# Moving one-hot compares between three engines in a two-layer graph network kernel

## What is computed

```python
h = relu(layernorm(x))                       # 256 x 512
adj[src, dst] = adj[dst, src] = 1.0          # 256 x 256, plus the identity
dinv = 1 / sqrt(adj.sum(1))
x = x + (adj * dinv[:, None] * dinv[None, :]) @ (h @ weight) + bias
h = relu(layernorm(x))
hs, hv = h[:, :128] @ w_in2f_s, h[:, 128:] @ w_in2f_v         # per node
s, v = hs[dst], hv[dst]                                       # gather to the edges
Wij = (ssp(edge_attr_20 @ W1 + b1) @ W2 + b2) * edge_weight   # per edge
agg = segment_sum(products of (s, v, edge_attr_4, Wij), src)  # scatter to the nodes
x = x + output_layers(agg)
```

## Time and profile before

| | |
|---|---|
| median of 3 runs | 71.9 us (71.62 to 71.95) |
| the profiled execution | 71.83 us, of which 69.8 us are the span of the profile |
| PE busy | 61.7 us (88%) |
| PEld busy | 48.6 us (70%) |
| DVE busy | 60.1 us (86%) |
| ACT busy | 48.6 us (70%) |
| POOL busy | 39.5 us (57%) |

### The profile page before, as it was taken

The page is one execution under the profiler, slowest core; times in us unless marked ns, Lnnn a source line. Parts: engine busy times, 40 slices in busy tenths (PEclk is TensorE's granted clock), DMA queues, the critical chain, the costliest instruction groups (busy, mean ns, idle before and its releaser), DMA issues.

```text
span 69.8 us, 1215 instructions
## 1 busy us (share of the span) xinstructions
PE 61.7 (88%) x407; PEld 48.6 (70%) x407; DVE 60.1 (86%) x124; ACT 48.6 (70%) x74; POOL 39.5 (57%) x46
## 2 busy tenths in 40 slices
PE   3999998999999999897998979999999999998340
PEld 1236754568834268796987969998898989997220
DVE  4599999999979968989999898989898999972760
ACT  0700059978999697967979999988696969732700
POOL 5000030000676989594799979999999988700000
PEclk9999999999999999999999999999999999999995
DMA  0899998984000000000000000000000000000044
GB/s 1 129 396 247 361 499 379 449 317 124 9 0 0 0 0 0 0 0 5 0 0 0 0 0 9 5 0 0 0 0 0 0 0 9 0 0 0 0 148 153
DMA packets 3049, 5.65 MB, mean 81 GB/s; under 512 B 540, under 2 KB 1936, under 8 KB 2916
## 3 DMA queue, kind: packets, MB, share of 16 engines
q1 hardware_dynamic: 2274, 5.14, 21.3%
q10 hardware_dynamic: 770, 0.44, 2.2%
HBM read 5.06 MB, written 0.52 MB: 80 GB/s over the span
## 4 chain that ended last, share of the span: by engine, by line
DVE 45%; PE 20%; issue 14%; ACT 13%; DMA 3%; DVEq 0%; ACTq 0%
ACT OsR L240 8%; DVE WQ L412 7%; DVE Os L412 7%; PE pair L632 5%; ACT w_sb L284 5%; DVE dst_bc L565 4%; PE pair L733 4%; PE pair L742 4%; DVE pair L514 3%; PE pair L674 3%; DMA idx_sb<-idx 3%; PE pair L721 3%; DVE w_sb L485 2%; DVE za L446 2%; DVE hX L449 2%
## 5 line engine op out<-in xcount | busy, mean ns | idle before, releaser
L733 PE MATMUL pair<-OsR,Mh 128*128 128x256 f32 x56 | 13.6, 281 | 0.0
L733 PE MATMUL pair<-OsR,Ml 128*128 128x256 f32 x56 | 13.6, 281 | 0.0
L721 PE MATMUL pair<-HL,OdT 128*128 128x256 f32 x68 | 10.1, 289 | 1.6 <-DVE dst_bc L565 0.7
L395 POOL TENSOR_TENSOR Ml<-dst_bc,Mh 128x512 fp32r<-128x512 f32 x8 | 10.4, 1305 | 1.1 <-ACT Mh L301 1.0
L721 PEld LDWEIGHTS pair<-HL,OdT 128*128 128x128 f32 x68 | 8.6, 188 | 2.8 <-issue 2.8
L733 PEld LDWEIGHTS pair<-OsR,Ml 128*128 128x128 f32 x56 | 10.5, 188 | 0.0
L733 PEld LDWEIGHTS pair<-OsR,Mh 128*128 128x128 f32 x56 | 10.5, 188 | 0.0
L605 PEld LDWEIGHTS pair<-WQ,Os 128*128 128x128 bf16 x68 | 6.8, 104 | 4.0 <-DVE WQ L412 1.8
L605 PE MATMUL pair<-WQ,Os 128*128 128x256 bf16 x68 | 9.4, 297 | 0.2 <-DVE WQ L412 0.2
L399 POOL TENSOR_TENSOR Ml<-dst_bc,Mh 128x512 fp32r<-128x512 f32 x7 | 9.2, 1309 | 0.0
L240 ACT ACTIVATE OsR<-Os 128x1024 fp32r<-128x1024 bf16 (+1 forms) x9 | 9.0, 999 | 0.0
(11 more groups left out here) (122 smaller groups left out, 140.2 us busy)
## 6 DMA issues: line engine op xcount, KB each, us to landing
dst_bc<-dst_row SPq DMA_DIRECT2D x1, 2176.0 KB, 12.9
w_sb<-w SPq DMA_DIRECT2D x1, 1024.0 KB, 8.1
x_sb<-x SPq DMA_DIRECT2D x1, 512.0 KB, 4.4
out<-x_sb SPq DMA_DIRECT2D x2, 192.0 KB, 1.9
f_sb<-f_t SPq DMA_DIRECT2D x1, 378.0 KB
b_sb<-bias SPq DMA_DIRECT2D x1, 256.0 KB, 13.1
w_sb<-w ACTq DMA_DIRECT2D x1, 128.0 KB, 4.1
out<-x_sb ACTq DMA_DIRECT2D x1, 128.0 KB, 1.9
```

The source lines that it names most:

```text
L395: nc.gpsimd.tensor_tensor(Ml[:, o, 0:n, feats(1)], M[:, o, 0:n, feats(1)], Mh[:, o, 0:n, feats(1)].bitcast(fp32), ALU.subtract).then_inc(q ...
L721: last = nc.tensor.matmul(gpair[g % 2][:, j * 2 * C:(j + 1) * 2 * C], OdT[:, a, t * P:(t + 1) * P], HL[:, a, :, :], start=(a == 0), stop=( ...
L733: last = nc.tensor.matmul(bank[4 + b][:, 0:N], part[:, g % RG, j, feats(b)], OsR[:, g % RG, j, :], start=(TG * g + j == 0 and part is Mh), ...
```

## The change

1. **Adjacency.** VectorE makes one-hots for 30 tiles, in eight waves. ScalarE makes the last four (TA = 4): eight Abs of 256 columns into `dist` and two Relu of 1024 columns. `adjacency(range(TV, T))` stands between the two transposes of h1.
2. **Order on TensorE.** The softplus matmuls go ahead, with the DMA of `f_sb` ahead of x's. One step of `first_layer(1)` stands before the transposes of `CI`. The aggregation goes by node half first and by high and low part second.
3. **Order on VectorE.** `xb` goes ahead of `CI`. `hX`'s and `hY`'s remainders are cut into three pieces each, around and behind `A`.
4. **OdT.** ScalarE makes quarter 2 of half 1 alone, with Abs before and Relu after `hW_hi`. VectorE takes quarter 3 of half 1 as a fifth compare, and makes quarter 0 of half 1 between the sum of squares and `h2T`. GpSimd makes columns E/2 to 7E/8 of half 0 in two compares right behind `scales`, and the last eighth after VectorE's fifth compare. `gap` now lies in `h1`.
5. **Bias.** Two fp32r parts in 64 rows in place of three bf16 parts in 96. One part is made on ScalarE, one on GpSimd.
6. **ScalarE's order.** `y_blocks(0, free)` goes ahead of `hW_hi`, `wc_sb` ahead of `h2`, `w2_hi` behind Ln.

The diff, cut to its core:

```diff
-    WAVES = ((0, 2), (2, 6), (6, 12), (12, 20), (20, 28), (28, 32), (32, T))
+    TA = 4
+    TV = T - TA
+    WAVES = ((0, 2), (2, 4), (4, 8), (8, 12), (12, 14), (14, 20), (20, 28), (28, TV))
...
+        ones = sb("ones", [64, P], fp32r)
+        b2p = sb("b2p", [64, P], fp32r)
...
         sp: dma idx
+            sp.dma_start(f_sb[0:KF, :], f_t).then_inc(d_f, 16)
             sp.dma_start(x_sb[:, :, :], x.rearrange("(a p) d -> p a d", p=P)).then_inc(d_x, 16)
-            sp.dma_start(f_sb[0:KF, :], f_t).then_inc(d_f, 16)
...
         scalar
+            act.wait_ge(d_idx, 16)
+            nc.scalar.activation(negidx[:, :, :], idx_sb[:, :].rearrange("p (h t) -> p h t", h=2)[:, :, TV:T], ACT.Copy,
+                                 scale=-1.0).then_inc(q["negidx"], 1)
+            for h, into in enumerate((Os, Od)):
+                for i in range(TA):
+                    nc.scalar.activation(dist[:, h, i, :], iota_r[:], ACT.Abs, bias=negidx[:, h, i:i + 1]).then_inc(q["dist"], 1)
+                act.wait_ge(q["dist"], TA * (h + 1))
+                nc.scalar.activation(into[:, TV:T, :], dist[:, h, :, :], ACT.Relu, bias=one[:, 0:1],
+                                     scale=-1.0).then_inc(q["near"], 1)
             absolute(0)
...
-            nc.scalar.activation(gap, dst_bc[:, E // 2:], ACT.Abs, bias=iota_n[:, 1:2]).then_inc(q["gap"], 1)
-            nc.scalar.activation(OdT[:, 1, E // 2:], gap, ACT.Relu, bias=one[:, 0:1], scale=-1.0).then_inc(q["OdTa"], 1)
+            act.wait_ge(q["near"], 2)
+            act.wait_ge(q["adj"], 1)
+            act.wait_ge(q["y"], 1)
+            y_blocks(0, free)
+            nc.scalar.activation(gap, dst_bc[:, E // 2:3 * E // 4], ACT.Abs, bias=iota_n[:, 1:2]).then_inc(q["gap"], 1)
             (hW_hi, both halves)
+            nc.scalar.activation(OdT[:, 1, E // 2:3 * E // 4], gap, ACT.Relu, bias=one[:, 0:1],
+                                 scale=-1.0).then_inc(q["OdTa"], 1)
+            nc.scalar.activation(wc_sb[:], bank[1][:, 0:B], ACT.Copy, scale=SF * SB).then_inc(q["wcs"], 1)
...
         gpsimd
             pool.wait_ge(q["scales"], 2)
-            node_onehots_late(3)
+            node_onehots_late(E // 2, 3 * E // 4)
+            node_onehots_late(3 * E // 4, 7 * E // 8)
...
             scaled_late(1)
-            pool.wait_ge(q["OdT"], 4)
-            node_onehots_late(2)
+            pool.wait_ge(q["OdT"], 5)
+            node_onehots_late(7 * E // 8, E)
...
         vector
+            remainder_x(0)
+            remainder_x(1)
             dve.wait_ge(q["CT"], 1)
             (A, deg)
+            remainder_x(2)
             dve.wait_ge(q["hhi"], 2)
-            nc.vector.tensor_tensor(hY[0:64, :], za[64:128, :], hY[64:128, :].bitcast(fp32), ALU.subtract).then_inc(q["hYlo"], 1)
+            for c in range(3):
+                cols = slice(c * NG * P // 3, (c + 1) * NG * P // 3)
+                nc.vector.tensor_tensor(hY[0:64, cols], za[64:128, cols], hY[64:128, cols].bitcast(fp32),
+                                        ALU.subtract).then_inc(q["hYlo"], 1)
...
                                            accum_out=sq[:, 1:2]).then_inc(q["sq1"], 1)
+            node_onehots(1, 0)
             dve.wait_ge(q["tp2"], 2)
             (h2T, half 1)
-            for a in range(NH):
-                node_onehots(a, 0)
+            node_onehots(0, 0)
+            node_onehots(0, 1)
             (HL, low part)
-            for a in range(NH):
-                node_onehots(a, 1)
+            node_onehots(1, 1)
+            node_onehots(1, 3)
...
         tensor
+            adjacency(range(2, 4))
+            hidden(0)
+            hidden(1)
+            adjacency(range(4, 8))
+            hidden(2)
+            adjacency(range(8, 14))
+            transposed(0)
+            adjacency(range(TV, T))
+            transposed(1)
...
+            first_layer(1, 0, 1)
             (transposes of CI)
-            first_layer(1, 0, KD)
-            for p, (part, ready) in enumerate(((hW_hi, "hW_hi"), (hW_lo, "hW_lo"))):
-                for b in range(NH):
+            first_layer(1, 1, KD)
+            for b in range(NH):
+                for p, (part, ready) in enumerate(((hW_hi, "hW_hi"), (hW_lo, "hW_lo"))):
```

More of the change, by code:

```diff
@@ L92, in gnn_preln_kernel @@
         Od = flat[:, 0:T * N // 2].bitcast(bf16).rearrange("p (t n) -> p t n", t=T)
-        free = -(-(T * N // 2 + E // 4) // (7 * F))
-        gap = flat[:, T * N // 2:T * N // 2 + E // 4].bitcast(bf16)
+        free = -(-(T * N // 2 + TA * N) // (7 * F))
+        dist = flat[:, T * N // 2:T * N // 2 + TA * N].bitcast(bf16).rearrange("p (h t n) -> p h t n", h=2, t=TA)
         OsR = sb("OsR", [P, RG, TG, N], fp32r)
@@ L130, in gnn_preln_kernel @@
         Ml = sb("Ml", [P, RG, TG, S * F], fp32r)
+        gap = h1[:].rearrange("p a d -> p (a d)")[:, 0:E // 8].bitcast(bf16)
         aggT = b0_sb[:].rearrange("p (b n) -> p b n", b=2)
@@ L146, in gnn_preln_kernel @@
                  "h2 neg_h2 tp2 h2T0 h2T sq0 sq1 ve2 s2 H Hh Hl "
-                 "z zabs zexp zln hT hhi hXlo hYlo w2hi w2lo ones b2r b2p W Wsb "
-                 "y ybc WYp negc gap OdTa OdTp OdT OsR "
+                 "z zabs zexp zln hT hhi hXlo hYlo w2hi w2lo ones b2p W Wsb "
+                 "y ybc WYp negc negidx dist near gap OdTa OdTp OdT OsR "
                  "G Glo add vys Q svw red MA MhA MhB MlA MlB MlA_late MlB_late scat "
@@ L602, in adjacency @@
                 for t in ts:
-                    pe.wait_ge(q["onehot"], wave(t))
+                    if t < TV:
+                        pe.wait_ge(q["onehot"], wave(t))
+                    else:
+                        pe.wait_ge(q["near"], 2)
                     for a in range(NH):
                         last = nc.tensor.matmul(bank[4 + a][:, 0:N], Os[:, t, a * P:(a + 1) * P], Od[:, t, :],
-                                                start=(t == 0), stop=(t == T - 1))
-                if t == T - 1:
+                                                start=(t == 0), stop=(t == TV - 1))
+                if t == TV - 1:
                     last.then_inc(q["adj"], 1)
@@ L613, in hidden, with transposed @@
                 nc.tensor.matmul(zb[c][:, 0:hi - lo], w1_sb[:], f_sb[0:KF, lo:hi], start=True, stop=True).then_inc(q["z"], 1)
[L615 to L622, removed]
+            def transposed(a):
+                pe.wait_ge(q["eye"], NH + 1)
                 pe.wait_ge(q["h1"], a + 1)
@@ L648, in filters @@
                 ps = fbank[g][:, 0:n * P]
-                nc.tensor.matmul(ps, ones[:], b2p[:].unsqueeze(1).broadcast_to((96, n, P)), start=True, stop=False)
+                nc.tensor.matmul(ps, ones[:], b2p[:].unsqueeze(1).broadcast_to((64, n, P)), start=True, stop=False)
                 for i, stack in enumerate((hX, hY)[0:n // 2]):
@@ L657, in _ @@
             first_layer(0, 0, 2)
-            adjacency(range(12, 20))
+            adjacency(range(14, 20))
             first_layer(0, 2, 3)
-            adjacency(range(20, T))
+            adjacency(range(20, TV))
             first_layer(0, 3, KD)
+            first_layer(1, 0, 1)
             pe.wait_ge(q["CI"], NH)
@@ L714, in gather @@
                     pe.wait_ge(q["OdTa"], 1)
-                    pe.wait_ge(q["OdTp"], 2)
+                    pe.wait_ge(q["OdTp"], 1)
+                if (TG * g + tiles(g)) * P > 3 * E // 4:
+                    pe.wait_ge(q["OdT"], 5)
+                    pe.wait_ge(q["OdTp"], 3)
                 if g >= 2:
```

96 lines of the change are left out of this document (50 added, 46 removed).

## The result

The changed kernel takes 73.5 us (median of 4 runs, 73.09 to 73.8), against 71.8 us for the kernel before on the same chip. The ratio is 1.0239, with a 95% interval of 1.0195 to 1.0282: slower by 1.7 us. The profiled execution took 73.8 us, of which 71.8 are the span; the run before it to compare with took 71.83 and 69.8.

What follows compares the result with a forecast made beforehand. Bound: a chain through VectorE, TensorE and GpSimd, then VectorE to the edge loop. Terms −0.45 (adjacency), −0.55 (first power), +0.5 (fifth compare), +0.95 (h2 standing) net +0.45: 72.3 us, about 72.35 on the median; range 71.2 to 72.9.

Steps and rivals of the forecast that it cites:

- Direction: Whole kernel: the sum of gains and losses was put at +0.45 us, slower; chance of slower 0.51.
- early part: Up to x1: one-hots' 0.9 us becomes 0.45 at A, 0.55 more by the first power; x1 1.0 us earlier.
- The first power: GpSimd, ahead of `hW_hi`: beside a 0.45 us piece instead of xb's 1.22, it takes about 0.8 us; gain 0.55.
- the reading of the earlier trace: GpSimd stands while VectorE reads two SBUF tensors; the power ended 0.58 us after xb and itself needs about 0.6.
- The fifth compare: VectorE, x1 to the first row sum: one more compare, 0.74 us less up to 0.26 of idle time, +0.5.
- the bias: TensorE: nine bias matmuls change type, nothing to 0.2 us each, two ahead of h2's transposes; nothing, up to 0.4.
- h2's stall: VectorE's h2 of half 1 stands until GpSimd's second compare ends, as `ve` had behind GpSimd's y; +0.95 us.
- rival 1: VectorE's h2 doesn't stand behind GpSimd's compare: 71.4 us, 0.5 faster; chance 0.27.
- The rigid block: Everything behind the first row sum (33.56 us) keeps its length; only that start moves, to about 34.0.

Runs made afterwards that it cites:

- e6: Changed kernel with the bias of the kernel before, and xb's addition put back to right behind the degree: 73.78 us, ratio 1.0254 to the kernel before.
- e5: Changed kernel with the bias of the kernel before (three bf16 parts, 96 rows), run as a base for others: 71.53 us, ratio 0.9957 to the kernel before.
- e11: Kernel before with its bf16 bias matmul over 64 rows, the third bias part left out: 73.51 us, ratio 1.0165 to the kernel before.
- e3: Changed kernel with its fp32r bias padded by rows of zeros from 64 to 128 rows: 71.3 us, ratio 0.9943 to the kernel before.
- e2: Kernel before with only its bias changed to two fp32r parts in 64 rows: 73.62 us, ratio 1.0257 to the kernel before.
- e10: Changed kernel with its fp32r bias padded by rows of zeros from 64 to 96 rows: 71.5 us, ratio 0.9925 to the kernel before.
- e4: Changed kernel with its fp32r bias laid out four times in 512 columns: 74.41 us, ratio 1.0375 to the kernel before.
- e1: Changed kernel with the bias put back to three bf16 parts in 96 rows: median 72.29 us, no ratio taken.
- e7: Changed kernel with the bias of the kernel before, and ScalarE's four adjacency tiles given back to VectorE: 72.36 us, ratio 1.0101 to the kernel before.
- e9: Changed kernel with the earlier bias and VectorE's fifth compare cut into four pieces inside the edge loop: 71.9 us, ratio 1.0006 to the kernel before.
- e8: Changed kernel with the earlier bias, GpSimd's last compare no longer waiting for VectorE's fifth: 72.02 us, ratio 1.0054 to the kernel before.

## Why the prediction was wrong

**Direction and early part: right.** The working gave CI at 18.1, `hW_hi` at 22.2 and x1 at 25.3; the profile shows 18.00, 22.00 and 25.32. The first power took 1.03 us, not 0.8, but ended at 21.96, where 21.95 was forecast. Its end lies 0.58 us behind that of the piece of hX beside it, as it lay 0.58 behind xb's before and in e6 (22.38 against 21.80), so that the reading of the earlier trace rows held. What the reason leaves out is VectorE's own path: in e6, with xb behind the degree, `hW_hi` is 0.2 us later but `hW_lo`, and x1 with it, 0.8.

**The fifth compare: right in sum, in part by luck.** x1 to the first row sum was put at 7.75 us without a stall, and e5 measured 7.75. But its first compare took 0.90 us beside GpSimd's small instructions and not 0.74, and the two from 31.47 took 1.89 and not 1.47. These 0.6 us were not forecast, and more idle time of the kernel before went than the 0.26 us that the prediction took off, which made up for them.

**The failing step: the bias.** The prediction said "Nine bias matmuls change type" and bounded each between nothing and 0.2 us, "Nothing, up to 0.4" in all, and the sum has it at nothing. It looked at the type alone and not at the rows, 64 in place of 96. A filter group costs 0.41 us more: the type alone is 0.09 to 0.12, within the bound, and the rows, which the prediction gave no term, are 0.3 (e11, e3). It also counted only the two groups ahead of h2's transposes. One more stands ahead of the first gather and four between it and the third, where TensorE had rested 0.3 us ahead of the third gather. The bias alone is 1.8 us in e2, and taking it out gives e5 and e3 below the kernel before.

**The second failing step: h2's stall.** The prediction took 0.95 us, since `ve` had waited to GpSimd's end. h2 took 0.49 us in the middle of the compare. That the direction came out right is luck: the mechanism that was to give it wasn't there. With the bias put right, the change is rival 1's case: the prediction gave 71.4 for it, and e3 and e10 are at 71.3 and 71.5 (by their ratios 71.4 and 71.3).

**The rigid block.** The prediction took all behind the first row sum as one block. Four filter groups stand inside its start, between the first gather and the third. e2, which has neither the early gain nor the fall of the clock there, shows it alone: the first row sum is 0.5 us later than before (34.09), the third 1.3 (41.04).

**The clock.** No rival had it. It came in two of the four runs, for 0.6 us. The profiles of e4 and e10 (at about 31.8 and 31.5 us), e11 (32.0) and e6 (33.1) have it at this place too, and those of e1 to e3, e5 and e7 to e9 don't. So it came with 96 rows and with bf16, and stayed away in e2's profile with 64 rows of fp32r: a dearer filter phase isn't needed for it, and what starts it stays open.

The Trainium skill, SBUF — State Buffer, section "Who interferes with whom", has VectorE and GpSimd share a pair of ports that whichever instruction starts first keeps for its whole length, with the other fully blocked. The power beside xb (1.59 us against 1.03, e6) agrees with it. The changed kernel's h2, 0.49 us inside a compare of 1.64, does not, and in e8 neither compare lost the whole of the other; the measurement decides. For the weight load behind the bias, the Trainium skill, TensorE: Matmul & The Clock Gate, section "Step-by-step: what each phase is for", says that the load is pulled ahead of running matmuls where row groups don't conflict or it goes to the background buffer, and that the row count doesn't matter to the load's time. The loads' own times agree: 0.18 us for the 64 rows of the changed kernel's bias, 0.19 for the 128 of e3's. The pulling ahead shows in e3 (26.55 ahead of 26.67), but not around the 64-row matmul, where `w_hi`'s load stands for 0.24 us.

## What to carry to other kernels

When an operand gets smaller, look at what its neighbours lose: a matmul of 64 rows between matmuls of 128 cost 0.3 us a time, and zeros up to 96 rows made the changed kernel about 3% faster (e10), and 0.7% faster than the one before. Count every instruction whose form changes up to the next point where its engine is waited for, not only up to the first. And a wait on an engine is room for its own later work: xb in it was worth 0.8 us, while room in a loop that another engine keeps full is not room (e9).

## What the runs showed of the hardware

- The weight loads around a matmul of 64 rows among matmuls of 128 didn't move ahead, where those around one of 128 did (e3). Why is open. The price: 1.10 us a filter group with 64 rows of fp32r, 0.78 with 96 or 128; 0.98 with 64 rows of bf16, 0.69 with 96.
- A VectorE instruction (h2, one input in SBUF) that started 0.58 us into a GpSimd compare of 1.64 us kept its 0.49 us, and so it did in eight more profiles; one that started 1.04 us into the same compare took 0.89 (e6). A compare holds VectorE in some part of its time, and the two cases hint that it is the later one. That wasn't tried by itself.
- A GpSimd power of two columns took 1.03 us beside subtractions of 0.5 us and 1.59 beside one addition of 1.2 us, both with two SBUF inputs. Each time it ended 0.58 us after that instruction.
